# Starting eight feed-forward sums from VectorE, loading tiles ahead of weights, and halving the first and last tile of a three-stage layer

## The chip, the cores and the metric

One Trainium2 chip, one of its cores. The time is device microseconds for one launch. The kernel before was timed at 265.02 us, the median of 3 runs (264.71 to 265.19). Everything is float32.

The engines are named as the profile names them: PE is TensorE (PEld its weight loads), DVE is VectorE, ACT is ScalarE, POOL is GpSimd, SP is SyncE, which here only issues loads and stores.

## The reference

The input is 8 batches of 512 tokens with 128 channels. `ln` is a plain normalisation over the channels (mean 0, variance 1, epsilon 1e-5).

```
x  = hidden
n  = ln(x);  q = n @ Wq.T
x  = x + (q @ n.T) @ n                                   # no softmax
y  = ln(x);  h = relu(y @ w1 + b1);  z = h @ w2 + b2      # expert 0 only
x  = x + ln(y + z) * gamma + beta
t  = ln(x);  t = t + time_mix(ln1(t));  x = x + t + channel_mix(ln2(t))
y  = ln(x);  (the same feed-forward again)
x  = x + ln(y + z) * gamma + beta
```

time_mix is an RWKV mixer: three 128x128 products (k, v, r) of shifted tokens, three running scans over the 512 tokens, a sigmoid gate, and a fourth product. channel_mix is a product up to 512, a squared relu, a product back to 128, and a gate.

## The kernel before

Each batch is one tile of 128 partitions x (4 rows of 128 channels); the eight tiles `R[0]` to `R[7]` stay in SBUF the whole time. A matmul result fills one PSUM bank of 128x512; there are eight banks, and each call names the bank it uses. Attention has no softmax, so it is computed as n @ (Wq.T @ (n.T @ n)): `attn_gram` (n.T @ n), `attn_proj` (with Wq), `attn_transpose` (n.T), `attn_apply` (the last product). The two feed-forwards are called `f1` (after attention) and `f2` (last).

The order of the work is written out by hand. Each engine has its own program, which is a long list of calls such as `hidden_up(3, f2, 0, 4)` (batch 3, second feed-forward, hidden block 0, bank 4). An engine runs its list strictly in order, and a call waits on semaphores before it runs. The lists of all engines mix work of several batches, so that a batch in attention, one in time mixing and one in the second feed-forward run at once. The lists start near L370 for GpSimd, L693 for VectorE, L915 for ScalarE and L1142 for TensorE. SyncE issues all loads at the start (L233 to L254) and then the eight stores, each when its batch is ready.

One feed-forward of one batch goes like this. ScalarE normalises `R[b]` into `f_y` (`ffn_normed`, L758). TensorE transposes it (`ffn_transpose`, L993), and ScalarE copies the transposed tile to `f_yT`, adding the centred bias `B2C` per channel (`ffn_evacuate`, L813). TensorE makes four hidden blocks (`hidden_up`, L1032, two instructions each), and ScalarE applies bias and relu to each (`relu`, L821). TensorE then forms y + z in one bank: `ffn_start` (L1039) transposes `f_yT` back into the bank as the first term, with four instructions, and four `ffn_down` calls (L1048, eight instructions each) add the four hidden blocks. VectorE takes the statistics of the bank (`z_stats`, L422, and `mean_var`, L460), GpSimd computes the inverse root (`z_shift` L306, `power` L311), VectorE scales the sum (`ffn_scaled`, L497), and GpSimd adds it to `R[b]` with an accumulating DMA (`ffn_sum`, L356). For four batches of `f2` (1, 3, 5, 6) there is no `ffn_start`: a GpSimd DMA adds the bias rows `B2R` to `f_y` (`down_residual`, L348), and VectorE adds the bank to `f_y` (`z_sum`, L449). The sum of the last batch (`f2`, 7) is not moved by a DMA: `ffn_gain` (L475) and `ffn_out` (L483) add it on VectorE.

At the start, 24 transposes of the identity (`warm_up`, L1113) keep TensorE busy, then `centre_bias` (L1119) waits for the small tile `VEC`, then 20 more transposes follow, and then the first `attn_gram` (L1005). Meanwhile VectorE and GpSimd normalise the first tile (L422, L460, L284, L311, L658). `bias_part` (L1132) computes a bias for the hidden blocks (`B1C`) which the very first `relu` waits for.

Of the kernel before, what the change touches and what calls it, by code (L numbers as in the profile page):

```python
# [27 lines left out]
def hybrid_layer(nc, hidden, w_q, w1, w2, b1, wk, wv, wr, wo, f_wk, f_wr, f_wv, vectors, gamma, beta, out):  # L28
# [5 lines left out]
    with ExitStack() as ctx:  # L34
# [6 lines left out]
        class Steps:  # L41


            def __init__(self, name, tiles, *steps):
                self.sems = [sem(f"{name}{n}" if tiles > 1 else name) for n in range(tiles)]
                self.steps = {s: n + 1 for n, s in enumerate(steps)}

# [3 lines left out]
            def done(self, b, step):  # L51
                return self.sem(b), len(self.steps) * (b // len(self.sems)) + self.steps[step]
# [65 lines left out]
        first_loaded, w1_loaded, w2_loaded = sem("first_loaded"), sem("w1_loaded"), sem("w2_loaded")  # L118
        gamma_loaded, tmix_loaded, cmix_loaded = sem("gamma_loaded"), sem("tmix_loaded"), sem("cmix_loaded")
        const_ready, ident_ready, pads_ready = sem("const_ready"), sem("ident_ready"), sem("pads_ready")  # L120
        decay_exp, decay_ready, decay_row = sem("decay_exp"), sem("decay_ready"), sem("decay_row")
        w2_stats_done, w2_mv_ready, w2_centred = sem("w2_stats_done"), sem("w2_mv_ready"), sem("w2_centred")
        b2_mean_psum, b2_centred, b1_part_psum, b1_ready = sem("b2_mean_psum"), sem("b2_centred"), sem("b1_part_psum"), sem("b1_ready")

        diag_ready, b2_rows_psum, b2_rows = sem("diag_ready"), sem("b2_rows_psum"), sem("b2_rows")

        class Norm:


            def __init__(self, n, dst=None, dst_name="", steps=("ve", "rs", "nb")):  # L130
# [6 lines left out]
                self.scale = Steps(n + "_scale_steps", 2, *steps)  # L137
# [6 lines left out]
        class Ffn:  # L144


            def __init__(self, n, x):
# [18 lines left out]
        x0_loaded = [sem(f"x0_{n}_loaded") for n in range(BATCHES)]  # L166
        stored = sem("stored")
# [54 lines left out]
        def _(sp):  # L222
            x0_dram = hidden.rearrange("b (j p) c -> b p j c", p=P)
            out_dram = out.rearrange("b (j p) c -> b p j c", p=P)

            def load_x0(b):
                sp.dma_start(R[b][:], x0_dram[b]).then_inc(x0_loaded[b], DMA)
# [5 lines left out]
            load_x0(0)  # L233
            load_x0(1)
            sp.dma_start(Wq[:], w_q).then_inc(first_loaded, DMA)
            sp.dma_start(VEC[:], vectors).then_inc(first_loaded, DMA)
# [7 lines left out]
            sp.dma_start(BETA[:].rearrange("p j c -> p (j c)"), beta).then_inc(gamma_loaded, DMA)  # L244
            sp.dma_start(Wk[:], wk).then_inc(tmix_loaded, DMA)
# [15 lines left out]
        def _(pool):  # L261
# [15 lines left out]
            def shift(b, n):  # L277
# [996 lines left out]
```

## Time and profile before

| | |
|---|---|
| median of 3 runs | 265.02 us |
| the profiled execution | 266.14 us |
| its span in the profile | 264.3 us |
| PE busy | 255.3 us (97%) |
| DVE busy | 228.2 us (86%) |
| ACT busy | 227.2 us (86%) |
| POOL busy | 159.0 us (60%) |

Busy time is a share of the whole span. A matmul's end is modelled, and consecutive matmuls overlap in the record: a group "x32, 3.73 us" has a mean of 275 ns for one, yet their starts lie about 111 ns apart. So for PE the useful reading is how far apart the starts are and whether anything ended an idle time; the mean duration is not a price per instruction.

### The profile page before, as it was taken

The numbers are of one execution on the slowest core, as the hardware profiler recorded it, in microseconds if no ns is written. First come the engines' busy times: TensorE is split into PE (matmuls) and PEld (weight loads), VectorE is DVE, ScalarE is ACT, GpSimd is POOL, SyncE is SP. The second block draws the span as 40 slices with busy tenths as digits, with TensorE's granted clock in tenths as the row PEclk, the third lists the DMA queues.
The fourth block names the chain that finished last, engine by engine and source line by source line (L and its number), as shares of the span: only waits on it lengthen the run. The fifth ranks groups of instructions, "written<-read, shape, count | busy, mean of one in ns | idle before, by whom it ended". The sixth has DMA issues, their size and how long they took to land. (4 is left out here: it accounts for less than half of the span.)

```text
span 264.3 us, 5318 instructions
## 1 busy us (share of the span) xinstructions
PE 255.3 (97%) x1544; PEld 191.7 (73%) x1544; DVE 228.2 (86%) x748; ACT 227.2 (86%) x440; POOL 159.0 (60%) x298
## 2 busy tenths in 40 slices
PE   7999999999999999999999999999999999999990
PEld 7987886866876686776588658757778658678770
DVE  3498569999999999999999999999999998637443
ACT  1397988999999999999989999999989979895630
POOL 4457676482498179179659827956069637445641
PEclk9999999999999999999999999999999999999996
DMA  6930420203022226303704130622046744725574
GB/s 184 297 110 0 82 42 1 42 15 64 2 42 40 40 42 103 58 2 67 133 2 75 18 67 2 119 41 43 0 71 120 126 85 115 126 43 87 118 150 122
DMA packets 18316, 19.15 MB, mean 72 GB/s; under 512 B 1520, under 2 KB 11632, under 8 KB 18288
## 3 DMA queue, kind: packets, MB, share of 16 engines
q0 software_dynamic: 7056, 12.85, 28.4%
q1 hardware_dynamic: 11232, 5.97, 8.0%
q8 instruction: 12, 0.20, 0.3%
q14 instruction: 16, 0.13, 0.2%
HBM read 3.87 MB, written 2.10 MB: 23 GB/s over the span
## 5 line engine op out<-in xcount | busy, mean ns | idle before, releaser
L1048 PEld LDWEIGHTS bank<-W,f_h 128*128 128x128 f32 x512 | 61.9, 192 | 8.4 <-issue 6.7
L1048 PE MATMUL bank<-W,f_h 128*128 128x128 f32 x512 | 64.3, 275 | 0.0
L1032 PE MATMUL bank<-f_yT,W 128*128 128x512 f32 x128 | 62.3, 598 | 0.0
L821 ACT ACTIVATE f_h<-bank,B1C 128x512 f32<-128x512 f32 x64 | 41.6, 681 | 9.5 <-PE bank L1032 8.2
L1096 PEld LDWEIGHTS bank<-FWv,KK 128*128 128x128 f32 x256 | 31.7, 192 | 5.0 <-issue 3.6
L1096 PE MATMUL bank<-FWv,KK 128*128 128x128 f32 x256 | 33.6, 275 | 0.0
L1032 PEld LDWEIGHTS bank<-f_yT,W 128*128 128x128 f32 x128 | 21.1, 190 | 16.7 <-issue 7.7
L1090 PE MATMUL bank<-XK,FWk 128*128 128x512 f32 x64 | 30.7, 599 | 0.0
L758 ACT ACTIVATE f_y<-R,f_yn_nb,f_yn_rs 128x128 f32<-128x128 f32 x64 | 26.3, 488 | 0.2 <-POOL f_yn_nb L315 0.2
L878 ACT ACTIVATE KK<-bank 128x512 f32<-128x512 f32 x32 | 18.4, 592 | 2.4 <-PE bank L1090 2.3
L882 ACT ACTIVATE KK<-KK 128x512 f32<-128x512 f32 x32 | 19.5, 625 | 0.1
L311 POOL TENSOR_TENSOR f_zn_rs<-f_zn_ve,K_RSQRT 128x4 f32<-128x4 f32 x16 | 18.9, 1183 | 0.5
L311 POOL TENSOR_TENSOR f_yn_rs<-f_yn_ve,K_RSQRT 128x4 f32<-128x4 f32 x16 | 18.6, 1161 | 0.0
L1090 PEld LDWEIGHTS bank<-XK,FWk 128*128 128x128 f32 x64 | 10.9, 190 | 9.8 <-issue 5.3
L339 POOL DMA_DIRECT2D R<-BETA x16 | 15.0, 964 | 4.6 <-ACT f_y L758 3.1
L293 POOL TENSOR_TENSOR tmix_tmp<-tmix_mv,K_EPS 128x4 f32<-128x4 f32 x8 | 2.5, 310 | 25.4 <-DVE tmix_mv L460 25.4
L306 POOL TENSOR_TENSOR f_zn_ve<-f_zn_mv,K_EPS 128x4 f32<-128x4 f32 x16 | 7.5, 469 | 16.6 <-DVE f_zn_mv L460 16.6
L364 POOL DMA_DIRECT2D R<-G x7 | 7.4, 1050 | 14.7 <-DVE G L634 14.7
L422 DVE BATCH_NORM_STATS2 f_yn_stats<-R 128x6 f32<-128x128 f32 x64 | 13.8, 278 | 2.0 <-DMA R<-G 1.7
L758 ACT ACTIVATE N<-R,tmix_nb,tmix_rs 128x128 f32<-128x128 f32 x32 | 13.1, 482 | 0.9 <-POOL tmix_nb L315 0.9
L758 ACT ACTIVATE NC<-N,cmix_nb,cmix_rs 128x128 f32<-128x128 f32 x32 | 13.1, 483 | 0.0
L284 POOL TENSOR_TENSOR f_yn_ve<-f_yn_mv,K_EPS 128x4 f32<-128x4 f32 x16 | 4.3, 270 | 14.5 <-DVE f_yn_mv L460 14.4
(144 smaller groups left out, 655.2 us busy)
## 6 DMA issues: line engine op xcount, KB each, us to landing
R<-BETA POOLq DMA_DIRECT2D x16, 256.0 KB, 3.4
R<-f_zg POOLq DMA_DIRECT2D x10, 256.0 KB, 3.4
R<-in_hidden SPq DMA_DIRECT2D x8, 256.0 KB, 3.9
R<-N POOLq DMA_DIRECT2D x8, 256.0 KB, 3.6
out_x<-R SPq DMA_DIRECT2D x8, 256.0 KB, 2.3
R<-G POOLq DMA_DIRECT2D x7, 256.0 KB, 3.5
f_y<-B2R POOLq DMA_DIRECT2D x4, 256.0 KB, 5.7
R<-f_y POOLq DMA_DIRECT2D x4, 256.0 KB, 3.9
```

The lines of the kernel that those rows point to most:

```text
L306: pool.tensor_tensor(n.ve[b % 2][:], n.mv[b % 2][:, :, 1], K_EPS[:], ALU.add).then_inc(n.scale.sem(b), 1)
L311: pool.tensor_tensor(n.rs[b % 2][:], n.ve[b % 2][:], K_RSQRT[:], ALU.pow).then_inc(n.scale.sem(b), 1)
L339: pool.dma_start(R[b][:], BETA[:], accum_op=ALU.add).then_inc(*f.xb.step(b))
L422: last = v.bn_stats(n.stats[b % 2][:, j, :], src[:, j, :])
L758: done = a.activation(dst[:, j, :], src[:, j, :], ACT.Identity, scale=n.rs[b % 2][:, j:j + 1], bias=n.nb[b % 2][:, j:j + 1])
L821: a.activation(at(f.h, b)[:, n, :], banks[bank][:], ACT.Relu, bias=B1C[:, n:n + 1]).then_inc(f.h_ready[n], 1)
L878: a.activation(at(KK, b)[:, n, :], banks[bank][:], ACT.Relu).then_inc(square[n].sem(b), 1)
L882: a.activation(at(KK, b)[:, n, :], at(KK, b)[:, n, :], ACT.Square).then_inc(square[n].sem(b), 1)
L1032: t_.matmul(banks[bank][:], W1[:, n * P:(n + 1) * P], at(f.yT, b)[:], start=True, stop=True).then_inc(f.h_psum[n], 1)
L1048: last = t_.matmul(banks[bank][:, j * C:(j + 1) * C], at(f.h, b)[:, n, j * P:(j + 1) * P], W2[:, n, :], start=(n == 0 and j == 0 and b in ...
L1090: t_.matmul(banks[bank][:], FWk[:, n * P:(n + 1) * P], at(XK2, b)[:], start=True, stop=True).then_inc(kk_psum[n], 1)
L1096: last = t_.matmul(banks[bank][:, j * C:(j + 1) * C], at(KK, b)[:, n, j * P:(j + 1) * P], FWv[:, n, :], start=(n == 0 and j == 0), stop=(n ...
```

## The change

What it does, part by part:

1. For eight sums (`f1` batches 0 to 3, `f2` batches 4 to 7) VectorE writes `f_y` + `B2R` straight into the PSUM bank; TensorE's `ffn_down` products are then added onto it. For the other eight TensorE's `ffn_start` stays. `down_residual`, `z_sum` and their relatives are gone. In the eight, the hidden blocks take the raw bias `B1` and the transposed tile is copied without a bias. In the other products and transposes that fill a bank in four parts, only the first part now carries `start=True`, where all four did.
2. `B2R` is computed at the very start (`bias_rows`, `bias_rows_centred`); `bias_part` moves from the start to just before the hidden blocks of batch 3 of `f1`, in bank 0.
3. The warm-up is 10 real products on a zeroed tile (20 instructions) in place of 44 transposes; VectorE zeroes the tile first, and TensorE no longer waits for the identity before it.
4. The first tile is loaded as two halves, one from SyncE's queue and one from ScalarE's, with `VEC` behind it on ScalarE's; its statistics, inverse root and normalisation run half by half. Tiles 5, 6, 7 are loaded ahead of the time mixing weights.
5. The last batch of `f2` goes into two banks, two rows of 128 in each; its products of the blocks 2 and 3 are ordered by rows, and statistics, root, scaling, output and store run per half.
6. The rings `f1_h`, `f2_h` shrink from 2 to 1 copies and `f1_y`, `f2_y` from 4 to 3. All four lists of calls are written anew.

```diff
-COPIES = {"N": 3, "f1_y": 4, "f2_y": 4, "f1_yT": 2, "f2_yT": 2, "f1_h": 2, "f2_h": 2, "XN": 3, "XNT": 2, "GRAM": 2,
-          "PROJ": 2, "f1_zg": 3, "f2_zg": 3, "others": 1}
-IN_SBUF = {"f2": (1, 3, 5, 6)}
+COPIES = {"N": 3, "f1_y": 3, "f2_y": 3, "f1_yT": 2, "f2_yT": 2, "XN": 3, "XNT": 2, "GRAM": 2, "PROJ": 2,
+          "f1_zg": 3, "f2_zg": 3, "others": 1}
+STARTED = {"f1": (0, 1, 2, 3), "f2": (4, 5, 6, 7)}
+FIRST, LAST = ((0, 1), (2, 3)), ((0, 1), (2, 3))
...
# sync
-            load_x0(0)
+            load_rows(FIRST[0], x0_half)
             load_x0(1)
...
+                sp.wait_ge(*last[n].done(0, "out"))
+                sp.dma_start(out_dram[B - 1][:, rows[0]:rows[-1] + 1, :], R[B - 1][:, rows[0]:rows[-1] + 1, :]).then_inc(stored, DMA)
# vector
+            def ffn_start(b, f, bank, *free):
+                if b == f.started[0]:
+                    dve.wait_ge(*b2_rows.done(0, "centred"))
+                for s, count in free:
+                    dve.wait_ge(s, count)
+                dve.wait_ge(*f.norm.ready.done(b, "all"))
+                v.tensor_tensor(bank_rows(bank), at(f.y, b)[:], B2R[:].unsqueeze(1).broadcast_to([P, J, C]), ALU.add).then_inc(f.y_psum, 1)
...
+            warm_tile(); first_stats(0); first_mean_var(0); bias_diagonal(); first_stats(1); first_mean_var(1)
+            attn_stats(1); first_normed(0); first_normed(1); mean_var(1, na); attn_stats(2); mean_var(2, na)
+            bias_rows_centred(); attn_stats(3); attn_out(0, 0); mean_var(3, na); ffn_stats(0, f1)
...
+            ffn_scaled(6, f2, 0); last_stats(0, 7); last_mean_var(0); last_stats(1, 3); last_mean_var(1)
+            last_scaled(0, 7); last_scaled(1, 3); last_out(0); last_out(1)
# gpsimd, first and last lines of its list
+            first_shift(0); first_power(0); first_shift(1); first_power(1); shift(1, na); power(1, na); bias(1, na)
...
+            last_shift(0); last_power(0); last_shift(1); last_power(1)
# scalar
+                bias = B1 if b in f.started else B1C
...
+            act.dma_start(R[0][:, FIRST[1][0]:, :], hidden.rearrange("b (j p) c -> b p j c", p=P)[0][:, FIRST[1][0]:, :]).then_inc(x0_loaded[0], DMA)
+            act.dma_start(VEC[:], vectors).then_inc(vec_loaded, DMA)
# tensor
-                    last = t_.matmul(banks[bank][:, j * C:(j + 1) * C], at(f.h, b)[:, n, j * P:(j + 1) * P], W2[:, n, :], start=(n == 0 and j == 0 and b in f.in_sbuf),
+                    last = t_.matmul(banks[bank][:, j * C:(j + 1) * C], at(f.h, b)[:, n, j * P:(j + 1) * P], W2[:, n, :], start=False,
...
+            def last_down(part, bank):
+                for n in (2, 3):
+                    pe.wait_ge(f2.h_ready[n], B)
+                for j in LAST[part]:
+                    for n in (2, 3):
+                        done = t_.matmul(banks[bank][:, j * C:(j + 1) * C], at(f2.h, B - 1)[:, n, j * P:(j + 1) * P], W2[:, n, :], start=False,
+                                         stop=(n == H - 1), skip_group_check=True)
+                done.then_inc(last[part].sem(0), 1)
...
             def warm_up(bank, count):
+                pe.wait_ge(*warm.done(0, "tile"))
                 for _ in range(count):
-                    t_.transpose(banks[bank][:, 0:P], IDENT[:], IDENT[:])
+                    last = t_.matmul(banks[bank][:, 0:P], WROW[:, 0:P], WROW[:, 0:P], start=True, stop=True)
+                last.then_inc(warm.sem(0), 1)
...
+            warm_up(0, 10)
             pe.wait_ge(ident_ready, 1)
-            warm_up(0, 24); centre_bias(); warm_up(0, 20); attn_gram(0, 0); attn_transpose(0, 1); attn_proj(0, 0)
-            bias_part(); attn_apply(0, 0); attn_transpose(1, 1); attn_gram(1, 2); attn_transpose(2, 0, x1.ready(0))
+            bias_rows(); attn_gram(0, 0); attn_transpose(0, 1); attn_proj(0, 0); attn_apply(0, 0)
+            attn_transpose(1, 1); attn_gram(1, 7, b2_rows.done(0, "column")); attn_transpose(2, 0, x1.ready(0))
...
+            hidden_up(7, f2, 2, 2, (f2.h_ready[3], 8)); last_down_first(0, 7, 3); last_down_first(1, 7, 3)
+            last_down(0, 7); last_down(1, 3)
```

## Rows read from the trace of the kernel before

**Rows 1.** Busy time in three stretches: stretch, length, each engine busy (instructions), clock, DMA.

```profile
0.00:44.00 44.00, 42.08 (x283) 35.87 (x284) 29.58 (x162) 30.48 (x74) 26.22 (x78) 1.00 0.42 107
44.00:215.00 171.00, 170.90 (x1005) 124.01 (x1004) 170.08 (x475) 166.10 (x308) 109.81 (x183) 1.00 0.30 53
215.00:264.30 49.30, 42.28 (x260) 31.80 (x258) 28.59 (x113) 30.66 (x59) 22.97 (x38) 0.96 0.54 108
```

**Rows 2.** Waits of PE: who it waited for, us in total, times, longest.

```profile
PE bank L1113 <- POOL IDENT L264: 1.5, 1, 1.5
PE bank L993 <- ACT XN L758: 0.3, 1, 0.3
```

**Rows 3.** Busy time in two other stretches, columns as in rows 1.

```profile
9.40:17.00 7.60, 7.21 (x62) 6.61 (x60) 4.10 (x25) 6.25 (x18) 4.03 (x10) 1.00 0.88 252
17.00:257.30 240.30, 240.18 (x1442) 177.19 (x1440) 215.84 (x679) 219.70 (x423) 148.73 (x260) 1.00 0.33 60
```

**Rows 4.** Timeline, start of the kernel: start us, us, engine, line, operation.

```profile
0.74 0.98 SPq L227 DMA_DIRECT2D R<-in_hidden  x2
1.53 5.38 PE L1113 MATMUL bank<-IDENT 128*128 128x128 f32 x24 [1.53 <-POOL IDENT L264]
...
2.32 0.43 SPq L236 DMA_DIRECT2D VEC<-in_vectors  x1
...
3.54 0.87 DVE L422 BATCH_NORM_STATS2 attn_stats<-R 128x6 f32<-128x128 f32 x4 [3.54 <-DMA R<-in_hidden]
...
4.45 0.38 DVE L460 BATCH_NORM_AGGREGATE attn_mv<-attn_stats 128x2 f32<-128x6 f32 x4
...
4.99 0.20 POOL L284 TENSOR_TENSOR attn_ve<-attn_mv,K_EPS 128x4 f32<-128x4 f32 x1 [3.02 <-DVE attn_mv L460]
...
5.29 1.03 POOL L311 TENSOR_TENSOR attn_rs<-attn_ve,K_RSQRT 128x4 f32<-128x4 f32 x1
...
6.43 1.11 DVE L658 TENSOR_SCALAR XN<-R,attn_mv,attn_rs 128x128 f32<-128x128 f32 x4 [0.43 <-POOL attn_rs L311]
...
6.71 0.43 PE L1119 MATMUL bank<-VEC,MEAN 128*128 128x1 f32 x2
...
7.00 2.67 PE L1113 MATMUL bank<-IDENT 128*128 128x128 f32 x20
...
9.50 1.06 PE L1005 MATMUL bank<-XN 128*128 128x128 f32 x8
...
11.31 0.95 PE L1132 MATMUL bank<-B2C,W 128*128 128x1 f32 x8
```

**Rows 5.** Timeline of the last products of PE and what follows them.

```profile
251.40 0.60 PE L1039 MATMUL bank<-IDENT,f_yT 128*128 128x128 f32 x4
...
253.55 3.73 PE L1048 MATMUL bank<-W,f_h 128*128 128x128 f32 x32
...
257.32 0.89 DVE L422 BATCH_NORM_STATS2 f_zn_stats<-bank 128x6 f32<-128x128 f32 x4 [2.78 <-PE bank L1048]
258.25 0.38 DVE L460 BATCH_NORM_AGGREGATE f_zn_mv<-f_zn_stats 128x2 f32<-128x6 f32 x4
258.54 0.66 DVE L475 TENSOR_TENSOR f_zg<-bank,GAMMA 128x512 f32<-128x512 f32 x1
258.71 0.20 POOL L306 TENSOR_TENSOR f_zn_ve<-f_zn_mv,K_EPS 128x4 f32<-128x4 f32 x1 [3.01 <-DVE f_zn_mv L460]
258.98 1.03 POOL L311 TENSOR_TENSOR f_zn_rs<-f_zn_ve,K_RSQRT 128x4 f32<-128x4 f32 x1
260.05 1.14 DVE L483 SCALAR_TENSOR_TENSOR R<-f_zg,f_zn_rs,R 128x128 f32<-128x128 f32 x4 [0.85 <-POOL f_zn_rs L311]
```

**Rows 6.** DMA issues by kind: count, KB each, median us from issue to landing.

```profile
out_x<-R SPq DMA_DIRECT2D x8, 256.0 KB, 2.3
R<-in_hidden SPq DMA_DIRECT2D x8, 256.0 KB, 3.9
VEC<-in_vectors SPq DMA_DIRECT2D x1, 6.0 KB, 2.9
```

**Rows 7.** Groups by shape, DVE: count, busy us, mean ns, idle before.

```profile
L466 DVE TENSOR_TENSOR R<-bank,R 128x512 f32<-128x512 f32 x8 | 5.4, 681 | 5.3 <-PE bank L1020 5.2
L449 DVE TENSOR_TENSOR f_y<-bank,f_y 128x512 f32<-128x512 f32 x4 | 2.7, 671 | 3.8 <-PE bank L1048 3.8
```

**Rows 8.** Waits of ACT: who it waited for, us in total, times, longest.

```profile
ACT f_h L821 <- PE bank L1032: 8.2, 5, 2.8
ACT f_h L821 <- DVE B1C L681: 1.3, 1, 1.3
```

**Rows 9.** The relu of the hidden blocks: duration ns min/median/max, first and last start.

```profile
L821 ACT ACTIVATE f_h<-bank,B1C x64: 665/680/710, 23.2 to 254.0; 128x512 f32<-128x512 f32 x64
```

More of the change, by code:

```diff
@@ L51, in done @@
             def done(self, b, step):
-                return self.sem(b), len(self.steps) * (b // len(self.sems)) + self.steps[step]
+                less = self.less if b and b % len(self.sems) == 0 else 0
+                return self.sem(b), len(self.steps) * (b // len(self.sems)) + self.steps[step] - less
         class Rows:
@@ new lines, in last_start, with warm_tile @@
+            def last_start(part, bank, *free):
+                for s, count in free:
+                    dve.wait_ge(s, count)
+                dve.wait_ge(*f2.norm.ready.done(B - 1, "all"))
+                c = slice(LAST[part][0], LAST[part][-1] + 1)
+                v.tensor_tensor(bank_rows(bank)[:, c, :], at(f2.y, B - 1)[:, c, :], B2R[:].unsqueeze(1).broadcast_to([P, len(LAST[part]), C]),
+                                ALU.add).then_inc(f2.y_psum, 1)
+            def warm_tile():
+                v.memset(WROW[:], 0.0).then_inc(warm.sem(0), 1)
@@ L663, in centre_down_weights, with up_bias @@
+            def up_bias(bank):
+                dve.wait_ge(b1_part_psum, 1)
+                dve.wait_ge(w1_loaded, 2 * DMA)
+                v.tensor_tensor(B1C[:], B1[:], banks[bank][:, 0:H], ALU.subtract).then_inc(b1_ready, 1)
             def centre_down_weights():
@@ L1129, in bias_part @@
+            def bias_part(bank, *free):
                 pe.wait_ge(w1_loaded, 2 * DMA)
[L1130 removed]
+                freed(free)
+                pe.wait_ge(*b2_rows.done(0, "column"))
                 for n in range(H):
[L1132 removed]
+                    last = t_.matmul(banks[bank][:, n:n + 1], W1[:, n * P:(n + 1) * P], B2C[:], start=True, stop=True)
                 last.then_inc(b1_part_psum, 1)
[L1135 removed]
@@ L1235, in _, with ffn_start @@
-            ffn_down(6, f2, 1, 6); ffn_transpose(7, f2, 5); ffn_down(6, f2, 2, 6); ffn_down(6, f2, 3, 6)
-            hidden_up(7, f2, 0, 5); hidden_up(7, f2, 3, 4); ffn_start(7, f2, 6, (f2.z_ready, 4))
-            hidden_up(7, f2, 1, 5, (f2.h_ready[0], 8)); hidden_up(7, f2, 2, 2); ffn_down(7, f2, 0, 6)
-            ffn_down(7, f2, 1, 6); ffn_down(7, f2, 2, 6); ffn_down(7, f2, 3, 6)
+            def ffn_start(b, f, bank, *free):
+                freed(free)
+                pe.wait_ge(f.yT_ready, b + 1)
+                for j in range(J):
+                    t_.matmul(banks[bank][:, j * C:(j + 1) * C], at(f.yT, b)[:, j * P:(j + 1) * P], IDENT[:], start=(j == 0), stop=False,
+                              is_transpose=True, skip_group_check=True)
@@ new lines, in _ @@
+            product_v(4, 3); ffn_transpose(0, f2, 2, (f1.h_ready[3], 8)); product_o(3, 4, (f1.h_ready[2], 8))
+            ffn_down(7, f1, 2, 6); ffn_down(7, f1, 3, 6); hidden_up(0, f2, 1, 2); tmix_transpose(5, 4, (u1_ready, 4))
+            cmix_up(2, 3, 7); hidden_up(0, f2, 0, 1, (f1.zg_ready, 7)); cmix_up(2, 0, 0)
+            product_r(4, 5, cgate.done(1, "kvs")); cmix_up(2, 1, 4, (xa_ready, 6))
+            hidden_up(0, f2, 2, 7, square[3].done(2, "relu")); ffn_start(0, f2, 1, (f2.h_ready[0], 1))
```

749 lines of the change are left out of this document (387 added, 362 removed).

## The prediction, made before the change was run

> **What bounds the kernel now.** I read the busy shares by stretch first [rows 1]. From 44 to 215 us TensorE is busy 170.9 us of 171, VectorE 170.1 and ScalarE 166.1: three engines are full at once, so shares alone don't name the bound. Then I read who waited for whom. TensorE has two recorded waits in the whole kernel, 1.5 us for the identity at the start and 0.3 us once [rows 2], and from 17 us to the end of its last product it is busy 240.18 of 240.30 us [rows 3]. Its record of busy time is modelled, so I checked the spacing: 32 products of 128 columns take 3.73 us, or (3.73 - 0.28) / 31 = 0.111 us from start to start, and four transposes take 0.60 us, or (0.60 - 0.27) / 3 = 0.109 us [rows 5]. That is back to back, at the upper level of the clock. VectorE on the other hand has 14.4 us of idle time before 44 us and 20.7 after 215 [rows 1]. So TensorE sets the time from its first useful product to its last, and the span has three parts:
>
> - the head, until the first product of attention starts at 9.50 us [rows 4];
> - TensorE's stream, 9.50 to 257.3 us [rows 4, 5];
> - the tail behind its last product: statistics, inverse root, output and store, 257.3 to 264.3 us [rows 5].
>
> A change pays here if it starts the stream earlier, takes an instruction off TensorE, or shortens the tail. Work that is put on VectorE costs nothing outside 44 to 215 us.
>
> **The change, part by part.**
>
> Head. Before, the normalised first tile is there at 6.43 + 1.11 = 7.54 us, but TensorE starts on it only at 9.50, since the second warm-up (20 transposes, 2.67 us) stands in its list behind the wait for `VEC` [rows 4]. Now the warm-up is 20 instructions. At the spacing of the first warm-up, 5.38 / 24 = 0.224 us, they take 4.5 us, and start at about 1.3 us (a 0.5 us fill that VectorE begins at 0.75, an estimate from the start of the other engines at 0.74). They and the four bias products (at most 0.9 us) end at about 6.7. The chain of the data decides. The whole tile lands 2.8 us after its issue (0.74 to 3.54). For half I take 3.3 us; the bounds are 3.54 and 3.04, the latter from the quickest landing there is, 2.3 us for a store [rows 6]. Then two of four statistics (0.87 / 2), two aggregations (0.2), hand-over: 4.0. GpSimd's shift 0.2 and root 1.03: 5.3. The second half's shift and root follow on the same engine: 6.6. The second half's scaling on VectorE is 1.11 / 2 and a hand-over: 7.3 us. So the first product starts at 7.3 in place of 9.50: **-2.2 us**. The root of a 128x2 tile has no row. If it costs half of the 128x4 one, the chain ends at 6.7 or earlier, so the warm-up and bias products bound at 6.7 (-2.8). If `VEC` lands only at 5.2 as now (2.32 + 2.9 [rows 4, 6]), `bias_diagonal` holds the second half's statistics behind it on VectorE, everything comes 0.8 us later (-1.4). I keep -1.4 to -2.8.
>
> The Trainium skill, "DMA: Bandwidth & Descriptors", section "Issuing engines are not separate DMA queues", speaks against the two queues: both run on the same 16 DMA engines, and only the issuing time is saved. By that rule both halves land together, at 3.5 us instead of 3.3, and the sum would be 0.2 us less.
>
> What stood in a gap. The eight products of `bias_part` (0.95 us) lie between two steps of the first batch, while ScalarE copies [rows 4]. They filled a gap; now the gap stays empty and they stand in the full stream at batch 3: **+0.8 us** (0 to 0.95). In return the first relu no longer waits for `B1C` on VectorE, 1.3 us on ScalarE [rows 8]; TensorE had no wait of that time, so I count nothing (0 to -0.5).
>
> TensorE's stream. `ffn_start` on TensorE goes from 12 to 8 batches: f1 loses four (0 to 3), f2 loses 4 and 7 but gains 1 and 3. Four times four transposes of 0.109 us: **-1.75 us**. The two products of `down_bias_part` leave the stream: **-0.2**. The start flags cost nothing; the number of instructions is the same.
>
> VectorE. Eight `ffn_start` there have no row (a sum of two SBUF tiles written to PSUM); the nearest are sums of the same size with one operand in PSUM, 0.671 and 0.681 us [rows 7]. I take 0.68, bounds 0.6 and 0.75. That adds 8 x 0.68 = 5.4 us and takes away the four `z_sum`, 2.7. Of the added, the first of f1 and those of f2 4 to 7 fall where VectorE has room (14.4 and 20.7 us); about two (f1 2 and 3) fall at the edge of the full stretch, from which one or two `z_sum` go. I count 0 on the sum; that cover is gone if VectorE is what sets the time, the second rival. ScalarE's work hardly changes. GpSimd loses four DMA issues and queues less.
>
> The shorter rings. With one copy of the hidden blocks, the first `relu` of a feed-forward waits until the last `ffn_down` of the one before it is done; behind it in ScalarE's list everything waits. In the lists as written other `hidden_up` calls stand beside the last downs, so that the banks are filled meanwhile; I count 0. The other end is the first relu's 0.68 us [rows 9] at every hand-over.
>
> Tail. Now 3.87 us lie between the start of the last statistics, 257.32, and the end of the output, 261.19 [rows 5]. In two halves: the first half's products end 8 x 0.111 = 0.9 us ahead of the last. Counted from the end of the last product: the second half's statistics 0.45, aggregation 0.2, hand-over; GpSimd's first root (1.03) started at about 0 and ends at about 1.05; shift and second root end at 2.35; the second output 1.14 / 2 ends at 2.95. The two scalings and the first output fit in front of it on VectorE. **-1.0 us**; -1.5 if the root of two columns costs less, -0.6 with longer hand-overs. The last store moves half the bytes: **-0.2** of the 2.3 us [rows 6] (0 to -0.5).
>
> Loads. Tiles 5 to 7 ahead of four weights of 64 KB: time mixing starts at about 41 us, the loads are issued in the first 12; nothing either way.
>
> Sum: -2.2 + 0.8 - 1.75 - 0.2 - 1.0 - 0.2 = -4.55 us. The profiled execution, 266.14 us (264.3 of span and 1.8 around it), becomes 261.6. It was 1.1 us above the median of the runs; the same difference on 265.02 gives **260.5 us**.
>
> **The rivals.**
>
> *The clock stays low in the head.* In the trace the first warm-up runs at 0.224 us per transpose, the second at 2.67 / 20 = 0.13 [rows 4]; the later spacing of 0.109 is half of it, so TensorE ran at the 1.2 GHz level at first and at 2.4 GHz before the first useful product, after some 6 us without a pause. Now the warm-up is shorter, and a pause of up to 0.6 us and small products come before the first batch. If the level is still low at 7.3 us, each of the instructions costs 0.11 us more; 62 of them stand between 9.4 and 17 us [rows 3], and where some 35 run low, with part of it in waits that are there anyway, that is +2.5 us: 263.0. All 62 would be +6.8 at most. For it: the shorter warm-up. Against it: it keeps TensorE busy nearly as long in total, and the first product comes early.
>
> The Trainium skill, "TensorE: Matmul & The Clock Gate", section "Part 4: PE-mode transpose", says that the transpose mode doesn't count as activity for the clock. By that rule the old warm-up could not have raised the level and the new one, of real products, does so sooner, which lowers this rival's chance. The trace does not agree in full: the level rose at about 7.5 us with nothing but transposes and two small products before it. I give the rule little weight.
>
> *VectorE sets the time in the middle.* Its stretch from 44 to 215 us has no gap [rows 1]. If that stretch is a chain of its own, TensorE's saved instructions only turn into waits behind it. The stretch starts earlier only by what VectorE itself gains in the head (about 1 us, less 0.8 for the bias rows), and its own work stays about equal; the tail's 1.2 us remain: 265.0 - 0.2 - 1.2 = 263.6. For it: the fullness. Against it: TensorE never waited for VectorE [rows 2].
>
> *The single copy of the hidden blocks makes it slower.* ScalarE has 4.9 us of slack in the 171 [rows 1]. Fourteen hand-overs from one feed-forward to the next remain. When each stops ScalarE, and then TensorE behind it, for t, the cost is 14 t; from t = 4.55 / 14 = 0.33 us on the gain is gone. With one relu each (0.68) it is +9.5 - 4.55: 270.0; with half of the hand-overs, 265.2; I put the case at 267. For it: the ring is halved on an engine that is full, and banks that VectorE begins early are held longer. Against it: the lists are ordered anew around it.
>
> That the change doesn't do what it says I can exclude: the removed transposes are counted in the code.
>
> **How the numbers follow.** Forecast 260.5, chance 0.57. Low clock 263.0, 0.16. VectorE bound 263.6, 0.15. Hand-overs 267, 0.12. Own range of the forecast: the bounds above added, and the unknown gaps of new lists, 258.3 to 262.3. A measurement of this kernel tells 0.2% (0.5 us) from no change. Faster by more than that: the whole forecast, most of the two middle rivals (0.28 of 0.31), little of the last (0.02): 0.87. Within: 0.04. Slower: 0.09. The range reaches up to the two middle rivals: 258.0 to 264.0.
>
> **What would show it.** The first product on `XN` at 7.3 us (6.7 to 8.1), at 0.111 us spacing. TensorE with 8 groups of `f_yT` transposes (32 instructions, not 48) and again next to no waits from 17 us on. VectorE's eight sums into a bank at 0.6 to 0.75 us. From the last product to the last store's issue 2.9 us, not 3.9. Wrong would be: products at 0.21 us after 7.3; waits of TensorE for `f_h` or of ScalarE's relu for the bank sum of the batch before; or a last product later than about 254.5 us.

## The result, and the profile after

The changed kernel is slower. Its median is 268.41 us (265.2 to 271.01), and that of the kernel before, run beside it, 266.13 us (264.59 to 267.56); the ratio is 1.0063, with a 95% interval of 1.0036 to 1.009. A second set gave 1.0095 (1.0063 to 1.0127). The forecast was 260.5 us, faster, with a range of 258.0 to 264.0. Medians are of all executions; the ratios leave out those more than 1.5% above the fastest of their kernel. The profiled execution took 268.51 us with a span of 266.7; the one before 266.14 and 264.3.

The two ends of the kernel did what was forecast. The timeline of the start (columns as in [rows 4]):

```profile
1.45 4.26 PE L1209 MATMUL bank<-WROW 128*128 128x128 f32 x20 [1.45 <-DVE WROW L719]
...
3.57 0.49 DVE L453 BATCH_NORM_STATS2 attn_stats<-R 128x6 f32<-128x128 f32 x2 [2.17 <-DMA R<-in_hidden]
...
4.77 0.71 POOL L308 TENSOR_TENSOR attn_rs<-attn_ve,K_RSQRT 128x2 f32<-128x2 f32 x1
...
5.89 0.69 POOL L308 TENSOR_TENSOR attn_rs<-attn_ve,K_RSQRT 128x2 f32<-128x2 f32 x1
6.21 1.10 DVE L473 TENSOR_SCALAR XN<-R,attn_mv,attn_rs 128x128 f32<-128x128 f32 x4
...
7.37 1.16 PE L1085 MATMUL bank<-XN 128*128 128x128 f32 x8 [1.31 <-DVE XN L473]
```

The first useful product starts at 7.37 us in place of 9.50 [rows 4], at the upper clock level (eight in 1.16 us). The timeline of the end, which answers to [rows 5]:

```profile
258.76 1.95 PE L1142 MATMUL bank<-W,f_h 128*128 128x128 f32 x16
...
260.75 0.49 DVE L453 BATCH_NORM_STATS2 f_zn_stats<-bank 128x6 f32<-128x128 f32 x2
...
262.02 0.69 POOL L308 TENSOR_TENSOR f_zn_rs<-f_zn_ve,K_RSQRT 128x2 f32<-128x2 f32 x1
262.15 1.21 DVE L499 SCALAR_TENSOR_TENSOR R<-f_zg,f_zn_rs,R 128x128 f32<-128x128 f32 x4
```

From the end of the products (258.76 + 1.95 = 260.71) to the end of the output (262.15 + 1.21 = 263.36) there are 2.65 us, where there were 3.9 [rows 5]. But the last product ends at 260.7, not at 257.3. What is between was forecast 1.15 us shorter and is 5.5 us longer (7.37 to 260.7 against 9.50 to 257.3): a miss of 6.7 us. The same stretches as [rows 1] and the second of [rows 3], in the same columns:

```profile
0.00:44.00 44.00, 40.64 (x255) 32.36 (x256) 35.46 (x168) 31.79 (x75) 27.82 (x77) 1.00 0.43 107
44.00:215.00 171.00, 167.78 (x972) 121.08 (x971) 164.97 (x465) 161.99 (x304) 112.91 (x177) 0.99 0.27 47
17.00:260.70 243.70, 240.37 (x1413) 175.00 (x1411) 215.08 (x679) 216.91 (x415) 154.75 (x255) 0.99 0.31 55
```

In the middle TensorE, VectorE and ScalarE are each 3 to 5 us less busy than before: they stand still together. GpSimd alone is busier: over the whole span 165.4 us with 296 instructions, against 159.0 with 298 before. So its instructions have become longer. The waits of TensorE (columns as in [rows 2]) name the place, and GpSimd's line 350, the small product that every normalisation needs, has its durations beside it (ns, min/median/max, first and last start), first before and then after:

```profile
PE bank L1072 <- ACT NC L836: 3.0, 2, 2.3
PE bank L1209 <- DVE WROW L719: 1.5, 1, 1.5
PE bank L1085 <- DVE XN L473: 1.3, 1, 1.3
PE bank L1100 <- ACT PROJ L881: 0.5, 1, 0.5
```

```profile
L315 POOL TENSOR_TENSOR cmix_nb<-cmix_nm,cmix_rs x8: 197/200/235, 73.7 to 225.3; 128x4 f32<-128x4 f32 x8
```

```profile
L350 POOL TENSOR_TENSOR cmix_nb<-cmix_nm,cmix_rs x8: 188/433/3074, 72.5 to 222.0; 128x4 f32<-128x4 f32 x8
```

The timeline around the longest, 157 to 167 us, shows the whole chain:

```profile
157.23 1.01 POOL L293 TENSOR_TENSOR cmix_ve<-cmix_mv,K_EPS 128x4 f32<-128x4 f32 x1 [0.74 <-DVE cmix_mv L531]
...
160.57 3.07 POOL L350 TENSOR_TENSOR cmix_nb<-cmix_nm,cmix_rs 128x4 f32<-128x4 f32 x1
160.63 1.22 DVE L639 TENSOR_TENSOR AB<-AB,EB 128x1024 f32<-128x1024 f32 x1
...
161.77 0.68 DVE L575 TENSOR_TENSOR DX<-XA 128x512 f32<-128x512 f32 x1
...
162.37 1.22 DVE L644 TENSOR_TENSOR EA<-AB,EA 128x1024 f32<-128x1024 f32 x1
...
163.74 1.65 ACT L836 ACTIVATE NC<-N,cmix_nb,cmix_rs 128x128 f32<-128x128 f32 x4 [2.85 <-POOL cmix_nb L350]
...
165.14 0.66 PE L1072 MATMUL bank<-IDENT,NC 128*128 128x128 f32 x4 [2.35 <-ACT NC L836]
...
166.59 0.69 DVE L650 SCALAR_TENSOR_TENSOR G<-G,EA 128x512 f32<-128x512 f32 x1 [2.71 <-ACT G L946]
```

An operation of 0.2 us takes 3.07 and ends at 163.64, just as the last of three VectorE instructions ends (163.59), each of which takes two operands from SBUF (for `DX` both are parts of `XA`). The kernel before has the same three instructions; new is only that the small operation stands beside them. ScalarE waits 2.85 us for it, TensorE 2.35 for ScalarE, and VectorE 2.71 for ScalarE's next. After that pause TensorE's granted clock is lower (stretch, length, busy as before, then the clock):

```profile
166.00:168.00 2.00, 2.00 (x12) 2.00 (x11) 1.41 (x3) 2.00 (x4) 1.56 (x3) 0.50 0.22 36
168.00:170.00 2.00, 2.00 (x15) 2.00 (x15) 1.80 (x3) 2.00 (x5) 0.56 (x1) 0.75 0.51 88
```

That is the 1.2 GHz level for some 3 us, worth 2 x 0.50 + 2 x 0.25 = 1.5 us. At 72.5 us the same operation took 1.52 us and cost TensorE 0.7. So about 2.35 + 1.5 + 0.7 = 4.5 us of the 6.7 us of the miss have a name in the trace; whether they can be had back is for a run to say.

The kernel before already had such stretched operations, in places where little waited for them. This is the same product of the feed-forward's normalisation:

```profile
L315 POOL TENSOR_TENSOR f_yn_nb<-f_yn_nm,f_yn_rs x16: 190/202/1772, 16.8 to 245.7; 128x4 f32<-128x4 f32 x16
```

ScalarE waited 0.2 us for it in all. So that a small GpSimd operation can take nine times its usual 0.2 us could be read before the change was run.

### The profile page after: what moved, and what is told of

Read it like the earlier page. It is cut to its first block, busy times and chain, and to the rows that moved or that the text cites. A ratio compares the mean times of both kernels' runs of the same rounds, so it can differ in the third digit from the quotient of the medians.

```text
span 266.7 us, 5279 instructions
## 1 busy us (share of the span) xinstructions
PE 254.1 (95%) x1504; PEld 187.7 (70%) x1504; DVE 230.3 (86%) x757; ACT 226.5 (85%) x439; POOL 165.4 (62%) x296
## 4 chain that ended last, share of the span: by engine, by line
PE 61%; DVE 14%; ACT 8%; issue 7%; POOL 6%; DMA 1%; ACTq 0%; DVEq 0%; POOLq 0%
PE bank L1113 14%; PE bank L1122 13%; PE bank L1184 9%; PE bank L1190 8%; PE bank L1072 5%; PE bank L1171 2%; PE bank L1201 2%; PE bank L1155 2%; POOL cmix_nb L350 2%; PE bank L1100 2%; PE bank L1085 1%; ACT NC L836 1%; DMA VEC<-in_vectors 1%; ACT N L836 1%; DVE f_zg L568 1%
## 5 line engine op out<-in xcount | busy, mean ns | idle before, releaser
L1122 PEld LDWEIGHTS bank<-W,f_h 128*128 128x128 f32 x480 | 59.1, 194 | 8.9 <-issue 8.6
L1122 PE MATMUL bank<-W,f_h 128*128 128x128 f32 x480 | 61.6, 278 | 0.1
L1184 PE MATMUL bank<-XK,FWk 128*128 128x512 f32 x64 | 31.8, 598 | 0.0
L836 ACT ACTIVATE f_y<-R,f_yn_nb,f_yn_rs 128x128 f32<-128x128 f32 x64 | 26.3, 485 | 4.6 <-POOL f_yn_nb L350 4.5
L903 ACT ACTIVATE f_h<-bank,B 128x512 f32<-128x512 f32 x32 | 20.9, 681 | 7.6 <-PE bank L1113 5.5
L293 POOL TENSOR_TENSOR f_yn_ve<-f_yn_mv,K_EPS 128x4 f32<-128x4 f32 x16 | 9.2, 575 | 28.4 <-DVE f_yn_mv L531 28.4
L903 ACT ACTIVATE f_h<-bank,B1C 128x512 f32<-128x512 f32 x32 | 21.4, 687 | 0.6 <-issue 0.5
L568 DVE SCALAR_TENSOR_TENSOR f_zg<-bank,f_zn_rs,GAMMA 128x128 f32<-128x128 f32 x56 | 15.6, 339 | 4.4 <-issue 4.4
L382 POOL DMA_DIRECT2D R<-f_zg x14 | 13.1, 939 | 9.5 <-DVE f_zg L568 9.0
L836 ACT ACTIVATE NC<-N,cmix_nb,cmix_rs 128x128 f32<-128x128 f32 x32 | 13.2, 489 | 4.3 <-POOL cmix_nb L350 4.3
L346 POOL TENSOR_TENSOR f_zn_rs<-f_zn_ve,K_RSQRT 128x4 f32<-128x4 f32 x15 | 16.0, 1064 | 0.9
L341 POOL TENSOR_TENSOR f_zn_ve<-f_zn_mv,K_EPS 128x4 f32<-128x4 f32 x15 | 5.3, 352 | 17.8 <-DVE f_zn_mv L531 17.7
```

Source lines behind the costliest of these rows:

```text
L346: pool.tensor_tensor(n.rs[b % 2][:], n.ve[b % 2][:], K_RSQRT[:], ALU.pow).then_inc(n.scale.sem(b), 1)
L568: last = v.scalar_tensor_tensor(zg[:, j, :], z[:, j, :], f.znorm.rs[b % 2][:, j:j + 1], GAMMA[:], ALU.mult, ALU.mult)
L836: done = a.activation(dst[:, j, :], src[:, j, :], ACT.Identity, scale=n.rs[b % 2][:, j:j + 1], bias=n.nb[b % 2][:, j:j + 1])
L903: a.activation(at(f.h, b)[:, n, :], banks[bank][:], ACT.Relu, bias=bias[:, n:n + 1]).then_inc(f.h_ready[n], 1)
L1122: last = t_.matmul(banks[bank][:, j * C:(j + 1) * C], at(f.h, b)[:, n, j * P:(j + 1) * P], W2[:, n, :], start=False, stop=(n == H - 1), sk ...
L1184: t_.matmul(banks[bank][:], FWk[:, n * P:(n + 1) * P], at(XK2, b)[:], start=True, stop=True).then_inc(kk_psum[n], 1)
```

## The experiments

All are compared with the kernel before, on the chip that ran them; experiments 9 to 11 ran on another chip than 1 to 8, so between these two groups only the ratios can be compared. "Head and tail" is the kernel of experiment 4.

**1. The changed kernel again**, unaltered.

> The changed kernel once more, unaltered. Theory A (a fixed weakness of the new lists: the transposes of the channel mixing of batch 4 come up before ScalarE has normalised it, because a small GpSimd operation before it, cmix_nb, is stretched beside VectorE): TensorE waits 1.5 to 3 us for NC near 163 us again, and the ratio to before is 1.004 to 1.012. Rival B (the wait was an accident of the one profiled execution): no wait over 1 us there, and the ratio still above 1, so the loss lies elsewhere.

Measured: 268.57 us, ratio 1.0095 (1.0063 to 1.0127). The waits are the same (`PE bank L1072 <- ACT NC L836` 3.0 us, longest 2.3). The profiled execution took 267.29 us and shows no low clock at 166 us: the pause is there without the drop, and the execution is 1.2 us shorter than the one profiled first (268.51). Nine of the 12 executions took 268.31 us or more, the other three 267.04 to 267.29. Whether the drop is what parts them isn't shown: the mean clock is lower in the nine (at most 0.991 against 0.994 to 0.996), but the executions of the kernel before, whose profile has no drop in the middle, range from 0.990 to 0.997. Nor is the pause shown in every execution: two of the 22 of the first set took 265.2 and 265.38 us.

**2. Rings as before.** `COPIES` of the changed kernel with `"f1_y": 4, "f2_y": 4, "f1_h": 2, "f2_h": 2` again.

> The changed kernel with the rings as before: two copies of the hidden blocks in each feed-forward, four of the normalised tile. Rival C (the single copy of the hidden blocks stops ScalarE at the hand-overs, the last rival of the prediction): 3 to 5 us faster than the changed kernel, ratio to before 0.990 or less. Theory A: within 0.3% of the changed kernel run beside it, since no long wait of the trace has to do with f_h.

Measured: 268.52 us, the median of the run beside it (268.57); waits 2.9 us, longest 2.2. The pause and the low clock behind it are there as before, so the single copy of the hidden blocks, my third rival, doesn't make them. But the ratio is 0.9994 (0.9949 to 1.0038) against 1.0095 (1.0063 to 1.0127). It rests on six executions: four of the 12 took 264.57 to 265.55 us, which none of experiment 1 did and two of 22 in the first set, and seven took 268.49 or more. That the shorter rings cost something beside the pause is not excluded.

**3. The consumer later.** On TensorE, `cmix_transpose(4, ...)` and `product_k(6, ...)` a few calls later:

```
-  hidden_up(1, f2, 2, 4, ...); cmix_transpose(4, ...); ffn_down(1, f2, 0, 3)
-  cmix_down(3, 2, 6); ffn_down(1, f2, 1, 3); product_k(6, ...); cmix_down(3, 3, 6)
+  hidden_up(1, f2, 2, 4, ...); ffn_down(1, f2, 0, 3); cmix_down(3, 2, 6); ffn_down(1, f2, 1, 3)
+  cmix_transpose(4, ...); cmix_down(3, 3, 6); product_k(6, ...)
```

> The changed kernel with one call moved in TensorE's list: cmix_transpose(4) stands three calls later, behind ffn_down(1, f2, 0), cmix_down(3, 2) and ffn_down(1, f2, 1), which is 2.7 us of work, and product_k(6) behind cmix_down(3, 3). Theory A: the wait of 2.35 us near 163 us and the stretch at the lower clock behind it (1.7 us) go: 2 to 4 us faster than the changed kernel, ratio to before about 0.993. Rival B: no change. Rival D (GpSimd, ScalarE and VectorE are late there as a whole, so the wait only moves behind the next call): under 1 us faster, with a new wait of TensorE within 5 us.

Measured: 267.46 us, ratio 1.005 (1.0025 to 1.0075). TensorE's waits in the place of the old one, then GpSimd's and ScalarE's instruction:

```profile
PE bank L1190 <- ACT KK L964: 1.1, 1, 1.1
PE bank L1072 <- ACT NC L836: 0.7, 1, 0.7
PE bank L1184 <- DVE XK L681: 0.7, 1, 0.7
```

```profile
160.57 3.07 POOL L350 TENSOR_TENSOR cmix_nb<-cmix_nm,cmix_rs 128x4 f32<-128x4 f32 x1
163.74 1.65 ACT L836 ACTIVATE NC<-N,cmix_nb,cmix_rs 128x128 f32<-128x128 f32 x4 [2.81 <-POOL cmix_nb L350]
```

TensorE's wait is only split into three (2.5 us in all), since ScalarE and VectorE still stand. Only about 1.1 us come back (ratio 1.005 against 1.0095). The order of TensorE's list at this place is not the cause.

**4. Head and tail alone.** The kernel before with the new start (tile in two halves on two queues, `WROW` warm-up, `VEC` early) and the new end (last sum two and two); sums, rings and the lists between as before:

```
-  load_x0(0)
+  sp.dma_start(R[0][:, 0:2, :], x0_dram[0][:, 0:2, :]).then_inc(x0_half, DMA)
-  shift(0, na); power(0, na); bias(0, na); ...
+  first_shift(0); first_power(0); first_shift(1); first_power(1); ...
-  ...; z_shift(7, f2); power(7, f2.znorm)
+  ...; last_shift(0); last_power(0); last_shift(1); last_power(1)
```

> The kernel before, its lists and sums untouched, with the new head (first tile in two halves on two queues, warm-up of 10 products, VEC on ScalarE's queue) and the new tail (last sum in two banks, two rows each). If the prediction's terms hold where the lists stay: head -2.1 us, tail -1.0 us, so 2.5 to 3.3 us faster than before, ratio 0.988 to 0.991. If a gain in the head is swallowed by the full engines in the middle: only the tail's 1 us, ratio 0.996.

Measured: 263.37 us, ratio 0.9895 (0.9862 to 0.9929), 2.8 us faster than before and the fastest kernel here that leaves nothing out. Its first products:

```profile
6.82 2.07 PE L1102 MATMUL bank<-XN 128*128 128x128 f32 x8 [0.51 <-DVE XN L485]
```

They start earlier still, but run at the 1.2 GHz level (2.07 us for eight, against 1.16): here my first rival comes true, for 0.9 us in these eight and about 0.5 more in the four transposes behind them (1.06 us, against 0.60). Its middle, full as before [rows 1]:

```profile
44.00:215.00 171.00, 170.90 (x1001) 123.84 (x1001) 170.04 (x472) 165.24 (x306) 108.38 (x182) 1.00 0.31 54
```

With the old lists `cmix_nb` takes 197 to 236 ns there. Head and tail are right, and the loss is in the rest of the change: 268.4 - 263.4 = 5 us (4.5 to 5.3 by the ratios).

**5. The stretched operation on VectorE.** The changed kernel, with `cmix_nb` of batches 0 and 4 taken from GpSimd and put ahead of the first long VectorE product:

```
+  def bias_dve(b, n):
+      dve.wait_ge(*n.scale.done(b, "rs"))
+      v.tensor_tensor(n.nb[b % 2][:], n.nm[b % 2][:], n.rs[b % 2][:], ALU.mult).then_inc(n.scale.sem(b), 1)
-  ...; tmix_change(2); weighted(1); ...
+  ...; tmix_change(2); bias_dve(0, ncm); weighted(1); ...      (and bias_dve(4, ncm) ahead of weighted(5))
```

> The changed kernel, with one small operation of GpSimd (cmix_nb, 128x4) done on VectorE instead, for batches 0 and 4 alone: on VectorE it stands just ahead of the long sum of two SBUF tiles beside which it took 3.07 us on GpSimd, 0.2 us being usual. Theory A (that operation, stretched beside VectorE, holds ScalarE 2.9 us, and through it VectorE 2.7 and TensorE 2.35): ScalarE's waits for cmix_nb go from 3.8 us to under 1, TensorE's waits for NC from 3.0 to under 1, and the kernel is 2.5 to 4 us faster than the changed one, about level with before or a little under it (ratio 0.993 to 1.000). Rival D (everything is late there anyway): the waits move to other operations and the gain is under 1 us.

Measured: 264.92 us, ratio 0.9967 (0.9941 to 0.9994). That is 3.5 us under the changed kernel by the medians, and by the ratios 2.6 (against 1.0063) or 3.4 (against 1.0095), each about 1 us either way. The two operations take 0.16 us, no wait of TensorE for `NC` is left, and the profiled execution has no low clock in the middle. The stretch of 20 us around the stall, of the changed kernel and of this one:

```profile
155.00:175.00 20.00, 17.65 (x100) 13.50 (x99) 16.01 (x35) 16.23 (x32) 12.30 (x16) 0.91 0.31 53
```

```profile
155.00:175.00 20.00, 20.00 (x116) 14.12 (x115) 19.77 (x51) 19.81 (x37) 14.55 (x20) 1.00 0.31 54
```

VectorE does 51 instructions there in place of 35. Two instructions of 0.2 us on GpSimd, the engine with the most idle time, decide half or more of the 5 us.

**6. The sums of the changed kernel begun by TensorE.** Each `ffn_start` of VectorE's list put back as four transposes ahead of its first `ffn_down`; the sums' bias rows, which only VectorE's sum adds, are left out.

> The changed kernel with its eight sums begun by TensorE again (transposes of f_yT in front of the first product, 32 instructions more), nothing on VectorE for them. In these eight the feed-forward biases b1 and b2 are left out as far as they went through VectorE's sum. If TensorE sets the time, as the prediction has it: +3.5 us (8 x 0.44), 272 us. Rival E (VectorE's eight sums, 5.4 us of work, are what made the lists late): no slower than the changed kernel or faster.

Measured: 270.33 us, ratio 1.0183 (1.0143 to 1.0223), against 1.0063 and 1.0095 of the changed kernel: 3.2 or 2.3 us slower, each about 1 us either way. The stall and the low clock are there (2.8 us, longest 2.3). 32 transposes more are 32 x 0.109 = 3.5 us of TensorE. So VectorE's sums as such help in the changed kernel; whether by the full count isn't resolved.

**7. Two sums of the full kernel end on VectorE.** Head and tail, with `ffn_start(4, f2)` and the last start moved to VectorE, eight transposes (0.9 us) less on TensorE.

> The kernel before with the new head and tail, and VectorE begins two sums of the second feed-forward, batch 4 and batch 7 (two halves), in place of TensorE's transposes; both lie where VectorE has room. TensorE sets the time: -0.9 us (2 x 0.44) against the version with head and tail alone, ratio to before 0.986. Rival: 0, because what follows waits for VectorE.

Measured: 263.95 us, ratio 0.9935 (0.9907 to 0.9963), against 263.37 and 0.9895. In place of 0.9 us less there are 1.1 us more, 1.2 either way: no gain. Only one of the two stood where VectorE had room (248.8 us); the sum of batch 4 started at 209.0, and from 205 to 212 us VectorE was busy 7.00 us of 7.

**8. Six sums in the full stretch on VectorE.** Head and tail, with f1 4 to 7 and f2 0 and 2 begun by VectorE: 24 transposes (2.6 us) less on TensorE, six sums (6 x 0.68 = 4.1 us) more on VectorE.

> The kernel before with the new head and tail, and VectorE begins the six sums of f1 4 to 7 and f2 0 and 2, all in the stretch where VectorE has no gap. TensorE does 24 transposes less (-2.6 us), VectorE 4.1 us more. TensorE sets the time and VectorE has a backlog that costs nothing: ratio 0.980. VectorE sets it in that stretch (second rival of the prediction): up to 4 us slower than head and tail alone, ratio about 1.004, with waits of TensorE for VectorE.

Measured: 267.08 us, ratio 1.0045 (1.002 to 1.007): 3.7 us slower than head and tail (4.0 by the ratios).

```profile
44.00:215.00 171.00, 166.91 (x950) 117.70 (x949) 169.02 (x473) 162.43 (x299) 108.58 (x177) 1.00 0.30 52
```

```profile
PE bank L1223 <- DVE G L709: 1.4, 2, 1.2
PE bank L1122 <- DVE N L717: 0.5, 1, 0.5
PE bank L1149 <- DVE f_zg L608: 0.4, 1, 0.4
```

TensorE, which never waited for VectorE in the kernel before [rows 2], now has 4 us of gaps (171 less 166.91), and its recorded waits name VectorE. It looked like proof that VectorE sets the time. The next three put a price on each engine.

**9. TensorE's starts twice.** Head and tail, with six `ffn_start` between 44 and 215 us issued twice, VectorE untouched:

```
-  ffn_start(4, f1, 0, ...)
+  ffn_start(4, f1, 0, ...); ffn_start(4, f1, 0)          (and so for f1 5, 6, 7 and f2 0, 2)
```

> The kernel of the head-and-tail experiment (263.37 us, ratio 0.9895), with TensorE's transposes that begin a feed-forward sum done twice for six batches between 44 and 215 us (first feed-forward 4 to 7, second 0 and 2): 24 transposes more, 24 x 0.109 = 2.6 us of TensorE, the result unaltered, all other engines' work untouched. TensorE sets the time in the middle (the forecast's view): +2.6 us, 266.0, ratio near 1.000. VectorE sets the time and TensorE has slack behind it: 263.4 to 264.0, ratio 0.990 to 0.992. Both share it: 264.7.

Measured: 265.07 us, ratio 0.9939 (0.991 to 0.9968) against 0.9895: +0.0044 x 266 = +1.2 us for 2.6 us of TensorE, 1.2 either way.

**10. Less on VectorE.** Head and tail, `mix_r` on 128 of 512 columns (the other three quarters of the gate's input are left out):

```
-  v.scalar_tensor_tensor(at(DX, b)[:], at(DX, b)[:], vec("mix_r"), at(XA, b)[:, 0:T], ...)
+  v.scalar_tensor_tensor(at(DX, b)[:, 0:P], at(DX, b)[:, 0:P], vec("mix_r"), at(XA, b)[:, 0:P], ...)
```

> The head-and-tail kernel with VectorE's mix_r done on 128 of its 512 columns (the rest of the tile keeps the difference, so the gate's input is not the reference's for three quarters of the columns). From the rows of 128x512 (0.74 us) and 128x128 (0.34 us) of this operation: 8 x 0.40 = 3.2 us less on VectorE, all in the full stretch; TensorE's work is untouched. VectorE sets the time: up to -3.2 us, 260.2 to 261.4, ratio 0.978 to 0.982. TensorE sets the time: no change, 263.4. Both are near the bound and the other takes over at once: about 262.5.

Measured: 262.14 us, ratio 0.9838 (0.9804 to 0.9872) against 0.9895: -1.5 us for 3.2 us of VectorE (0.341 in place of 0.74 us, eight times), 1.3 either way.

**11. The same with the six sums of experiment 8.**

> The same 3.2 us taken off VectorE in the kernel in which VectorE begins six sums of the full stretch and TensorE has 24 transposes less (267.08 us, ratio 1.0045). VectorE sets the time: -3.2 us or a little more, 263.5 to 264. If the loss of that kernel came from waits that its placement makes and not from VectorE's total: 266 to 267. If TensorE were the bound it would be below the one before it, 260 to 261.

Measured: 265.94 us, ratio 0.9977 (0.9945 to 1.0009) against 1.0045: -1.8 us for the same 3.2, 1.1 either way. Experiments 9 and 10 are both measured against the six executions of experiment 4. All three differences lie between the two pure answers, the first only just: it can't be told from nothing, but it is under 2.6 us. So neither engine alone sets the time in the middle, and a microsecond on either is worth about half of one, as an estimate with a wide margin. One thing 10 and 11 can't separate: `mix_r` takes two operands from SBUF, so a shorter one also holds GpSimd less (in 44 to 215 us GpSimd is busy 105.7 us in experiment 10 against 108.4 in 4). By these prices experiment 8 would cost 0.5 x 4.1 - 0.45 x 2.6 = 0.9 us; it cost 3.7. The other 3 us may come from where the sums stand (VectorE's later steps late in a list that was written for others); no run shows it.

**12. GpSimd beside VectorE, by itself.** A small kernel that leaves the whole computation out: 6 to 24 VectorE instructions of one kind, and beside them 14 GpSimd products of 128x4.

> A kernel of its own, which leaves the whole computation out and stores its input: VectorE works through stretches of 6 to 24 equal instructions, and beside each stretch GpSimd does 14 products of 128x4 (last: 4 inverse roots). Kinds in order: VectorE idle; one SBUF operand and a column (128x512); statistics of 128x128; SBUF and bank (128x512); two SBUF operands into a bank; two SBUF operands into SBUF; the same with a column as well; a scan of two SBUF operands; 128x1024 with two SBUF operands; the last again, beside roots. Theory one (a GpSimd instruction can't finish, or not start, while VectorE reads two SBUF operands): 0.2 us each beside the first four kinds, and up to the length of the VectorE instructions, 0.7 to 1.2 us each or one stretch for all of them, beside those with two SBUF operands; in the changed kernel one of 0.2 us took 3.07 beside three of these. Theory two (only the 128x1024 form or the scan does it): 0.2 us beside the 128x512 sums, long ones beside the last three kinds. Theory three (it comes from what GpSimd itself or its DMA issues do, and VectorE has no part in it): 0.2 us throughout.

Measured (one execution, span 73.5 us; GpSimd's line 65, count, ns min/median/max, first and last start), in this order beside: nothing; one SBUF tile and a column; statistics; SBUF and bank; two SBUF tiles to a bank; two SBUF tiles 128x512; the same with a column as well; scan; 128x1024; and roots beside 128x1024:

```profile
L65 POOL TENSOR_TENSOR SC<-SA,SB x14: 198/198/199, 3.9 to 5.9; 128x4 f32<-128x4 f32 x14
L65 POOL TENSOR_TENSOR SC<-SA,SB x14: 194/252/440, 6.8 to 10.3; 128x4 f32<-128x4 f32 x14
L65 POOL TENSOR_TENSOR SC<-SA,SB x14: 198/199/203, 11.0 to 12.9; 128x4 f32<-128x4 f32 x14
L65 POOL TENSOR_TENSOR SC<-SA,SB x14: 195/196/199, 16.2 to 18.2; 128x4 f32<-128x4 f32 x14
L65 POOL TENSOR_TENSOR SC<-SA,SB x14: 193/195/647, 21.2 to 25.3; 128x4 f32<-128x4 f32 x14
L65 POOL TENSOR_TENSOR SC<-SA,SB x14: 195/356/647, 26.3 to 31.3; 128x4 f32<-128x4 f32 x14
L65 POOL TENSOR_TENSOR SC<-SA,SB x14: 192/386/706, 32.4 to 37.9; 128x4 f32<-128x4 f32 x14
L65 POOL TENSOR_TENSOR SC<-SA,SB x14: 192/578/1160, 39.4 to 48.0; 128x4 f32<-128x4 f32 x14
L65 POOL TENSOR_TENSOR SC<-SA,SB x14: 195/622/1179, 49.6 to 58.3; 128x4 f32<-128x4 f32 x14
L65 POOL TENSOR_TENSOR SC<-SA,SB x4: 1157/1162/1861, 59.9 to 64.0; 128x4 f32<-128x4 f32 x4
```

Theory one holds but for one kind: beside one SBUF tile and a bank the product keeps its 0.2 us; beside two SBUF tiles it takes up to the length of VectorE's instruction (0.65 beside 0.68, 1.18 beside 1.22), while others of the same 14 pass in 0.2. The miss is the kind with one SBUF tile and a column, where theory one had 0.2 us and up to 0.44 was measured. The changed kernel's new sums, two SBUF tiles into a bank, can hold the product too (0.65 at most, 0.2 in the median). VectorE's own instructions are no longer here than in the kernel (1.22 us for 128x1024). No single product here was held over three instructions, as the one of 3.07 us was, so how GpSimd missed two openings stays open.

The Trainium skill, "SBUF — State Buffer", section "Who interferes with whom", says that a VectorE instruction with two SBUF inputs contends with a GpSimd instruction that reads SBUF, and one with at most one SBUF input doesn't, unless it runs in a 2-port perf mode. The measurement agrees for the kinds with two inputs, for the statistics and for SBUF and bank; whether the kind with a column ran in such a mode is not on record. The same section lets issue order decide who waits; in the trace GpSimd's operation started first (160.57 against 160.63) and was still the one held, so that sentence isn't borne out here.

## Why the prediction was wrong, step by step

- **"ScalarE's work hardly changes. GpSimd loses four DMA issues and queues less": the step that failed.** I priced GpSimd by its count and let its small products stand at 0.2 us wherever the new lists put them, though the trace of the kernel before had one of 1.77 us. In the new lists one stood beside three VectorE instructions with two SBUF operands, another beside the end of one and the whole of a second, and they took 3.07 and 1.52 us; TensorE stood 2.35 and 0.7 us behind them. Taking these two off GpSimd (experiment 5) returned 2.6 to 3.5 us of the 6.7.
- **Head, -2.2 us: right in the sum** (9.50 to 7.37), with errors in its terms that cancel. The first half tile was there at 3.57, not 3.3, no sooner than the whole, and the second half's statistics waited behind `DIAG` until 4.78; in return the roots of two columns took 0.70 instead of 1.03. So the exact hit is luck. The halves landed 2.8 and 3.1 us after their issues, close together, as the sentence of the Trainium skill that the prediction cites ("DMA: Bandwidth & Descriptors", "Issuing engines are not separate DMA queues") would have it. The clock was up at 7.37, so the first rival didn't hold in the changed kernel, while it did in experiment 4.
- **Tail, -1.0 and last store -0.2: right within 0.2 us.** Output end to span end is 3.3 us after 3.1, so the store gave nothing; the chain gave 1.2.
- **"Eight `ffn_start` ... I take 0.68": right in size**, 0.683 us each for the seven of 128x512. They also fell where VectorE had room: four start at 17.9 to 41.4 us, the others at 219.5 us and later, and one `z_sum` left the full stretch.
- **"So TensorE sets the time from its first useful product to its last": not borne out.** It was never idle, yet 2.6 us more on it cost 1.2 (0 to 2.4, experiment 9), and 3.2 us less on VectorE gave 1.5 to 1.8 (10, 11). [Rows 1] showed both full. So TensorE's saved transposes needn't count in full: near the end of the full kernel eight of them brought nothing (experiment 7, where one of the two sums fell into VectorE's full stretch).
- **Sum.** 6.7 us missed between first and last product: 2.6 to 3.5 shown by experiment 5; the rest, 3 to 4 us, is open. By an estimate, -1.15 us of TensorE's stream at half its price leaves 0.6 of it. The terms +0.8, -1.75 and -0.2 were not measured one by one. Experiment 5's trace has small gaps (waits of TensorE of 0.8 us for `f_yT` and 0.5 for `PROJ`), which none of my runs took away, and the shorter rings are not cleared. Other stretched products are an untested candidate: in experiment 5 GpSimd is still busy 165.1 us, and ScalarE waits 4.5 us for `f_yn_nb` and 2.0 for `tmix_nb`, where it waited 0.2 and 0.9 in the kernel before.
- **Rivals.** VectorE in the middle (263.6) was half right: it shares the bound. But the new sums don't stand in the middle, so this doesn't explain the loss. The single copy was the case on the slower side; experiment 2 shows that the pause isn't its doing, and leaves open whether it costs something else. The cause that is shown, a GpSimd operation held up beside VectorE, was in none.

## What to carry to other kernels

When an engine's list is reordered, ask of every small GpSimd instruction on a chain what VectorE does at that moment: beside instructions that read two SBUF tiles it lasted up to as long as one of them in experiment 12 and as long as three in the kernel, and what waited for it stood. If two engines are both full for a long stretch, as here, a saving on one of them may not count in full; price it by adding work to each in turn. And test ends and middle of a bundled change apart: here the ends alone were worth 2.8 us, and the middle took away 5.

## What the runs showed that I had not expected

- A GpSimd product of 128x4 goes from 0.20 to 3.07 us in the kernel, and to 0.65 or 1.18 us in a kernel of its own, by what VectorE runs beside it.
- A pause of TensorE of 2.2 to 2.35 us is followed by the 1.2 GHz level for some 3 us in three profiled executions (the changed kernel, experiments 2 and 6), and not in a fourth (experiment 1, a pause of 2.3).
- With the other half issued at the same time, half a tile lands no sooner than the whole: 3.57 us against 3.54 [rows 4].
- GpSimd's inverse root takes 1.03 us for four columns and 0.70 for two.
